# Second attention of a four-layer kernel: another order of its score maxima, with three PSUM banks for them

## The reference

```python
c_kv = hidden_states @ w_dkv.T
q = (hidden_states @ w_q.T).reshape(B, S, HEADS, HEAD_DIM)
k = (c_kv @ w_uk.T).reshape(B, S, HEADS, HEAD_DIM)
v = (c_kv @ w_uv.T).reshape(B, S, HEADS, HEAD_DIM)
scores = jnp.einsum('bqhd,bkhd->bhqk', q, k) * scale
scores = scores + alibi_bias(S)[None, None]
attn = jax.nn.softmax(scores, axis=-1)
out = jnp.einsum('bhqk,bkhd->bqhd', attn, v).reshape(B, S, HIDDEN)
return out @ w_o.T
```

## Time and profile before

| | us |
|---|---|
| median of 3 runs | 3481.03 (3480.75 to 3494.99) |
| profiled execution, its own time | 3483.64 |
| its span | 3482.0 |
| plain scores alone, 19 quads | 2607 to 2662 |
| plain and transposed together | 2662 to 3118 |
| transposed and products alone | 3118 to 3161 |
| PE, DVE, ACT busy, share of the span | 75%, 60%, 46% |
| mean granted clock of PE | 0.819 |

### The profile page before, as it was taken

How to read it: one execution, slowest core, us unless ns; L and a number is a source line. 1 busy time by engine, 2 the same in 40 slices (tenths; PEclk the granted TensorE clock), 3 DMA queues, 4 the chain that set the end, 5 groups by cost and what they waited for, 6 DMA issues and landing times. The chain is left out here.

```text
span 3482.0 us, 45060 instructions
## 1 busy us (share of the span) xinstructions
PE 2622.4 (75%) x12496; PEld 1651.7 (47%) x12497; DVE 2087.5 (60%) x4677; ACT 1584.9 (46%) x2875; POOL 465.3 (13%) x758
## 2 busy tenths in 40 slices
PE   5991069601689989998999999588249999997693
PEld 2330023201467767775777677455124444444452
DVE  3338953598267767775777777532317776763422
ACT  2446324660256555664655566223112666664231
POOL 0220012100011111101111110031300000000314
PEclk8555555555699999999999999789675999998797
DMA  3000000001300000000000000222270022000123
GB/s 98 0 0 0 0 0 0 0 0 39 110 10 7 7 9 9 7 6 11 7 7 7 10 7 1 73 80 78 67 172 8 2 37 37 1 1 2 61 82 100
DMA packets 82226, 100.62 MB, mean 29 GB/s; under 512 B 24931, under 2 KB 71619, under 8 KB 79043
## 3 DMA queue, kind: packets, MB, share of 16 engines
q1 hardware_dynamic: 69476, 70.45, 7.8%
q0 software_dynamic: 12544, 27.68, 2.5%
HBM read 60.99 MB, written 36.70 MB: 28 GB/s over the span
## 5 line engine op out<-in xcount | busy, mean ns | idle before, releaser
L1122 ACT ACTIVATE aa_pt_hi<-psum 128x512 fp32r<-128x512 f32 x544 | 322.3, 595 | 343.5 <-PE psum L1028 342.8
L1662 DVE TENSOR_REDUCE ab_part_max<-psum 128x1 f32<-128x512 f32 (+3 forms) x640 | 364.2, 607 | 177.4 <-PE psum L1500 172.7
L1184 DVE TENSOR_TENSOR aa_pt_lo<-psum,aa_pt_hi 128x512 fp32r<-128x512 f32 x544 | 368.1, 687 | 39.6 <-ACT aa_pt_hi L1122 38.8
L1604 ACT ACTIVATE ab_prob<-psum 128x512 f32<-128x512 f32 (+3 forms) x640 | 303.5, 537 | 165.3 <-PE psum L1529 161.9
L1171 DVE CUSTOM_DVE_ANT_0 aa_prob<-psum,bias 128x512 f32<-128x512 f32 (+2 forms) x480 | 284.1, 597 | 108.1 <-PE psum L1018 102.4
L1500 PE MATMUL psum<-ab_k_stack,ab_q_stack 49*128 49x512 f32 (+3 forms) x640 | 285.4, 489 | 26.4 <-DVE ab_part_max L1662 25.8
L973 POOL TENSOR_TENSOR aa_tmp<-aa_q_nat,rope 128x128 f32<-128x128 f32 x256 | 109.1, 458 | 1294.7 <-ACT aa_q_nat L1099 1294.7
L1016 PE MATMUL psum<-ka_hi,aa_q_hi 128*128 128x512 f32 (+3 forms) x640 | 272.9, 426 | 9.2 <-DVE aa_chunk_max L1171 8.0
L1039 PE MATMUL psum<-aa_pt_hi,c_stack 128*128 128x512 f32 x544 | 271.5, 499 | 2.6 <-DVE aa_pt_lo L1184 2.6
L1028 PE MATMUL psum<-ident,aa_prob 128*128 128x128 f32 x1600 | 264.7, 273 | 10.2 <-ACT aa_prob L1114 5.6
L504 PE MATMUL psum<-ix_bad_row,mean 128*128 128x1 f32 x4 | 1.2, 363 | 340.9 <-DVE ix_bad_row L631 340.9
(11 more groups left out here) (343 smaller groups left out, 4980.7 us busy)
## 6 DMA issues: line engine op xcount, KB each, us to landing
f_rows_in<-sent SPq DMA_DIRECT2D x80, 128.0 KB, 2.0
done<-f_rows_out POOLq DMA_DIRECT2D x80, 128.0 KB, 2.0
aa_xt<-xT_rows SPq DMA_DIRECT2D x64, 128.0 KB, 2.4
w<-in_w SPq DMA_DIRECT2D x6, 896.0 KB, 7.2
sent<-ixp_zeros SPq DMA_DIRECT2D x4, 1280.0 KB, 10.4
x<-in_hidden SPq DMA_DIRECT2D x2, 2048.0 KB, 9.1
ab_q_stack<-stash_q_hi SPq DMA_DIRECT2D x32, 128.0 KB, 9.9
ab_k_stack<-stash_k_hi SPq DMA_DIRECT2D x32, 128.0 KB, 11.2
```

The costliest lines, as they stand in the source:

```text
L1122: nc.scalar.activation(pt_hi[(TB[t] + j) % RING][:], turn_bank[(TB[t] + j) % RING], ACT.Copy).then_inc(pt_hi_done, 1)
L1184: nc.vector.tensor_tensor(pt_lo[ring][:], turn_bank[(TB[t] + j) % RING], pt_hi[ring][:].bitcast(F32), ALU.subtract).then_inc(pt_lo_done, 1)
L1604: nc.scalar.activation(prob[i % 2][h][:, 0:w], t_bank[slot % RING][:, 0:w], ACT.Exp).then_inc(t_taken, 1)
L1662: nc.vector.tensor_reduce(part_max[e % 2][:, 4 * h + t % 4, part:part + 1], s_bank[piece % 2][:, 0:w], AX.X, ALU.max).then_inc(s_used, 1)
```

## The change

The order is written anew. Plain scores no longer run a fixed 19 quads ahead but one event ahead: while the transposed quads of event e are worked on, the plain quads of event e + 1 are issued. `wanted(i)` spreads them evenly over the first quads of the event, and leaves the last three (AHEAD = 3; two in an event of four quads) for the way of the maxima; in those it lets at most two quads of event e + 2 begin. The turn of an event's maxima comes at the end of the step after the one in which its last plain score was issued. Where a step has more than four fresh pieces, the surplus is issued after its four transposed scores, ahead of the products of the quad before.

Even groups take their chunks upward (4, 8, 12, 16 quads), odd ones downward (16, 12, 8, 4), so that neighbouring events are of like size. Ahead of the first transposed score stand the plain scores of event 0 and of half of event 1, then the turn of event 0.

The plain scores have three banks and the results one. The first `weigh` of an event now waits for `keep` of the event just before.

```diff
-    RING = 4
-    LEAD = 19
+    RING, S_RING = 4, 3
+    AHEAD = 3
+    EVENT = [(g, c) for g in range(NG) for c in (range(NCH) if g % 2 == 0 else reversed(range(NCH)))]
...
-        for m in range(LEAD):
-            steps += scores(m) + turns(m - 1)
+        def wanted(i):
+            e = T_QUADS[i][0]
+            if e + 1 == EVENTS:
+                return ALL
+            room = SIZE[e] - min(AHEAD, SIZE[e] // 2)
+            more = -(-(i - FIRST[e] + 1) * SIZE[e + 1] // room)
+            return FIRST[e + 1] + min(more, SIZE[e + 1] + AHEAD - 1)
+        turned = 0
+        steps += scores(SIZE[0])
         for i in range(ALL + 3):
-            fresh = scores(i + LEAD)
+            ready = issued
+            fresh = scores(wanted(i)) if i < ALL else []
+            if i == 0:
+                steps += fresh + [("turn", 0)]
+                turned, ready, fresh = 1, 0, []
             for h in range(GB):
                 if i < ALL:
                     steps.append(("t", i, h))
                 steps += fresh[h:h + 1]
+            steps += fresh[GB:]
             if 1 <= i <= ALL:
                 steps += [("weigh", i - 1, h) for h in range(GB)]
...
-            steps += turns(i + LEAD - 1)
+            if turned < EVENTS and FIRST[turned + 1] <= ready:
+                steps.append(("turn", turned))
+                turned += 1
...
-        s_bank, t_bank, o_bank = bank[0:2], bank[2:2 + RING], bank[6:8]
+        s_bank, t_bank, o_bank = bank[0:S_RING], bank[S_RING:S_RING + RING], bank[7]
...
-                    if piece >= 2:
-                        pe.wait_ge(s_used, piece - 1)
+                    if piece >= S_RING:
+                        pe.wait_ge(s_used, piece - S_RING + 1)
...
-                    if kb == 0 and h == 0 and e >= 2:
-                        pe.wait_ge(kept, e - 1)
+                    if kb == 0 and h == 0 and e:
+                        pe.wait_ge(kept, e)
```

More of the change, by code:

```diff
@@ L1348, in attention_b, with scores @@
     DEEP, LATE = 4, 5
-    RING = 4
-    LEAD = 19
[L1352 to L1357, removed]
-    def order():
[L1363 to L1369, removed]
-        for m in range(LEAD):
-            steps += scores(m) + turns(m - 1)
-        for i in range(ALL + 3):
-            fresh = scores(i + LEAD)
+    RING, S_RING = 4, 3
+    AHEAD = 3
+    EVENT = [(g, c) for g in range(NG) for c in (range(NCH) if g % 2 == 0 else reversed(range(NCH)))]
+    EVENTS = len(EVENT)
+    SIZE = [4 * (c + 1) for _, c in EVENT]
+    FIRST = [sum(SIZE[:e]) for e in range(EVENTS + 1)]
+    T_QUADS = [(e, g, c, kb) for e, (g, c) in enumerate(EVENT) for kb in range(4 * (c + 1))]
+    S_QUADS = [(e, g, t, part) for e, (g, c) in enumerate(EVENT) for t in range(4 * c, 4 * c + 4) for part in range(c + 1)]
+    ALL = len(T_QUADS)
+    NQ = ALL // NG
+    EVENT_ENDING = {FIRST[e + 1] - 1: e for e in range(EVENTS)}
+    def order():
+        steps, issued = [], 0
+        def scores(upto):
+            nonlocal issued
+            fresh = []
+            while issued < min(upto, ALL):
+                fresh += [("s", issued, h) for h in (1, 0, 3, 2)]
+                issued += 1
+            return fresh
+        def wanted(i):
[7 more added lines that the diff above has]
+        steps += scores(SIZE[0])
+        for i in range(ALL + 3):
+            ready = issued
[3 more added lines that the diff above has]
+                turned, ready, fresh = 1, 0, []
             for h in range(GB):
@@ L1378, in order @@
                 steps += fresh[h:h + 1]
+            steps += fresh[GB:]
             if 1 <= i <= ALL:
                 steps += [("weigh", i - 1, h) for h in range(GB)]
-                if (i - 1) % NQ in ENDS:
-                    steps.append(("keep", (i - 1) // NQ * NCH + ENDS.index((i - 1) % NQ)))
-            steps += turns(i + LEAD - 1)
-            if i >= 2 and (i - 2) % NQ in ENDS and (i - 2) // NQ < NG:
-                steps.append(("flip", (i - 2) // NQ * NCH + ENDS.index((i - 2) % NQ)))
+                if i - 1 in EVENT_ENDING:
+                    steps.append(("keep", EVENT_ENDING[i - 1]))
+            if turned < EVENTS and FIRST[turned + 1] <= ready:
+                steps.append(("turn", turned))
+                turned += 1
+            if i >= 2 and i - 2 in EVENT_ENDING:
+                steps.append(("flip", EVENT_ENDING[i - 2]))
         return steps
@@ L1474, in _ @@
                 for e in range(EVENTS):
-                    g, c = divmod(e, NCH)
+                    g, c = EVENT[e]
                     pool.wait_ge(t_taken, SLOT[("turn", e)] + 1)
@@ L1484, in score @@
                 def score(m, h):
-                    g, (t, part) = m // NQ, S_QUADS[m % NQ]
+                    e, g, t, part = S_QUADS[m]
                     w, piece = min(CH, (t + 1) * P - part * CH), PIECE[("s", m, h)]
-                    out, at = s_bank[piece % 2], slice(base(h), base(h) + R_MAX)
+                    out, at = s_bank[piece % S_RING], slice(base(h), base(h) + R_MAX)
                     q, k = q_stack[g % 2][h // 2], k_stack[g % 2][h // 2]
@@ L1511, in transposed_score @@
                 def transposed_score(i, h):
-                    g, (c, kb) = i // NQ, T_QUADS[i % NQ]
+                    e, g, c, kb = T_QUADS[i]
                     q0 = max(c * CH, kb * P)
@@ L1518, in transposed_score @@
                     if kb == 0 and h == 0:
-                        e = g * NCH + c
                         pe.wait_ge(max_in[e % 2], (e // 2 + 1) * GB * 16)
@@ L1532, in weigh @@
                 def weigh(i, h):
-                    g, (c, kb) = i // NQ, T_QUADS[i % NQ]
-                    e, q0 = g * NCH + c, max(c * CH, kb * P)
+                    e, g, c, kb = T_QUADS[i]
+                    q0 = max(c * CH, kb * P)
                     w = (c + 1) * CH - q0
                     pe.wait_ge(t_taken, SLOT[("t", i, h)] + 1)
-                    if kb == 0 and h == 0 and e >= 2:
-                        pe.wait_ge(kept, e - 1)
+                    if kb == 0 and h == 0 and e:
+                        pe.wait_ge(kept, e)
                     at = q0 - c * CH
-                    last = nc.tensor.matmul(o_bank[e % 2][32 * h:32 * h + DHB + 1, at:at + w], values[:, g * GB + h, kb, :],
+                    last = nc.tensor.matmul(o_bank[32 * h:32 * h + DHB + 1, at:at + w], values[:, g * GB + h, kb, :],
                                             prob[i % 2][h][:, 0:w], start=kb == 0, stop=kb == 4 * c + 3,
@@ L1564, in out_tile @@
                     last.then_inc(out_done, 1)
-                pe.wait_ge(after_set, 4)
+                pe.wait_ge(after_set, 3)
                 pe.wait_ge(same_in, 2 * SAME_ROWS * 16)
@@ L1597, in exponential @@
                 def exponential(i, h):
-                    c, kb = T_QUADS[i % NQ]
+                    e, g, c, kb = T_QUADS[i]
                     w, slot = (c + 1) * CH - max(c * CH, kb * P), SLOT[("t", i, h)]
@@ L1615, in keep @@
                 def keep(e):
-                    g, c = divmod(e, NCH)
-                    act.wait_ge(pv_done, g * NQ + ENDS[c] + 1)
+                    act.wait_ge(pv_done, FIRST[e + 1])
                     if e >= 2:
                         act.wait_ge(t_ready, SLOT[("flip", e - 2)] + 1)
-                    nc.scalar.activation(o_rows[e % 2][:], o_bank[e % 2], ACT.Copy).then_inc(kept, 1)
+                    nc.scalar.activation(o_rows[e % 2][:], o_bank, ACT.Copy).then_inc(kept, 1)
                 def store_sums(e):
-                    (g, c), slot = divmod(e, NCH), SLOT[("flip", e)]
+                    (g, c), slot = EVENT[e], SLOT[("flip", e)]
                     act.wait_ge(t_ready, slot + 1)
@@ L1629, in store_sums @@
                                          ACT.Copy).then_inc(t_taken, 1)
-                act.wait_ge(after_set, 4)
+                act.wait_ge(after_set, 3)
                 for what in STEPS:
@@ L1652, in _ @@
                 nc.vector.tensor_copy(halves[:], prob[0][1][:, 0:2 * P].rearrange("p (a n) -> p a n", a=2)).then_inc(after_set, 1)
-                for p in range(2):
-                    nc.vector.memset(o_bank[p], 0.0).then_inc(after_set, 1)
+                nc.vector.memset(o_bank, 0.0).then_inc(after_set, 1)
                 def maxima(m, h):
-                    (t, part), piece = S_QUADS[m % NQ], PIECE[("s", m, h)]
-                    e = m // NQ * NCH + t // 4
+                    (e, g, t, part), piece = S_QUADS[m], PIECE[("s", m, h)]
                     w = min(CH, (t + 1) * P - part * CH)
                     dve.wait_ge(s_ready, piece + 1)
-                    nc.vector.tensor_reduce(part_max[e % 2][:, 4 * h + t % 4, part:part + 1], s_bank[piece % 2][:, 0:w],
+                    nc.vector.tensor_reduce(part_max[e % 2][:, 4 * h + t % 4, part:part + 1], s_bank[piece % S_RING][:, 0:w],
                                             AX.X, ALU.max).then_inc(s_used, 1)
-                    if m % NQ in ENDS and h == 2:
+                    if m in EVENT_ENDING and h == 2:
```

## The result

The changed kernel takes 3502.54 us (median of 11 runs, 3494.26 to 3515.38), the kernel before 3483.57 in its 11. The ratio is 1.006, 95% interval 1.0043 to 1.0077: slower by 0.6%, 15 to 27 us. The profiled execution took 3507.04 us with a span of 3505.4.

The account below looks back on a forecast made before the run. PE and DVE hand two banks to and fro, neither full. After the start, 469.8 + 18 + 2.5 + 9 + 35 = 534 us against 499, begun 35 us earlier: change 0, 3480 us, range 3447 to 3512.

Parts of the forecast that it names:

- the clock: PE's clock in the phase: 111 us at half, costing 35 us, against 57 us costing 18 before.
- My prices of the steps: Steps after the start, priced by plain pieces and transposed width at full clock: 469.8 us in sum.
- 9 us of boundaries: Fifteen flips and turns between events cost PE 0.6 us each: 9 us, between 0 and 19.
- the nine waits for maxima: PE waits bare before events, 1.5 us six times and 3.0 three times; 8 us at half clock for each.
- The second rival: The clock stays down in the up-going runs of events: 3505 us, chance 0.15.
- The start: Plain scores ahead of the first transposed score: it comes at about 2626.5, 35.1 us earlier.
- A quad with three banks: Full step with one plain quad: 2.68 us in place of 3.33, as the third piece no longer waits.
- DVE-bound steps: Steps with two or more plain quads: DVE sets the pace, 2.58 us each plus 0.1.
- The rival that the bank does not help: The 44 one-quad steps stay at 3.33 us, costing 29 us more: 3509 us, chance 0.09.
- The count of the order: Steps priced by event: upward 18.4, 32.5, 43.8, 46.5 us, then downward 38.7, 28.0, 17.4, 11.7 in the first two groups.
- The way of the maxima: The 4.25 us from turn to transposed score, partly bare before nine events: 18 us together, plus 2.5 for a stage's DMAs.
- One result bank: Costs nothing, since products of the next event come late enough; without that cover 0.6 us x 15.

Follow-up runs that it names:

- the run with a lead of 17: Kernel before with three banks for plain scores and one for results, plain scores 17 quads ahead in place of 19: 3394.10 us, ratio 0.9769.
- Bursts: Old order, three banks for plain scores, 19 quads ahead, but two plain quads in every other step and none between: 3507.97 us in one run, against 3473.84 before.
- the two kernels with one plain quad a step: Three banks for plain scores, fixed 19 quads ahead: in the old order 3389.21 us, with the changed kernel's turned chunk order 3370.52 us.
- the experiment with the bank alone: Kernel before with three banks for plain scores and one for results, order untouched: 3389.21 us, ratio 0.9711.
- four banks: Four banks for plain scores, three for transposed ones, 19 quads ahead: old order 3386.67 us, even groups upward and odd ones downward 3381.02 us.
- three ways to put more work into PE: Changed kernel with off-diagonal plain scores' matmuls doubled: 3530.68 us; only 112 surplus ones: 3495.64 us; those 112 with an added 128-row matmul instead: 3520.99 us.
- all plain scores twice: Changed kernel with the matmul of each plain score off the diagonal issued twice into the same bank: 3530.68 us, ratio 1.0111.
- even groups, four banks: Even groups upward, odd ones downward, 19 quads ahead, four banks for plain scores and three for transposed ones: 3381.02 us, ratio 0.9735.
- these stacks were held back: Changed kernel, but DMAs bringing group 3's stacks wait until the maxima of event 9 have landed: 3504.61 us, ratio 1.0034.

## Why the prediction was wrong

I forecast no change, 3480 us, and it is 19 us slower. The step that failed is **the clock**: the prediction took 111 us at half, costing 35. There were 230. The price of 0.32 for a microsecond at half was near enough. My prices of the steps, 9 us of boundaries and 17 of waits leave 61 us of the 557 for the clock, 0.27 each. Steps of one kind, sorted by their plain pieces and the width of their transposed scores and set side by side at the two clocks, give 0.31 (55 us for 178 at half). So the 230 us cost some 60 to 70, an estimate. The term is 25 to 35 us short, and that is the miss.

I had tied the falls to the nine waits for maxima, because the fall that I looked at, at 3126, stood behind one. It was not the only one in the profile before. The earlier trace rows themselves lie in another, and in the 12 us ahead of that one PE never waited longer than 0.4 us:

```profile
2930.00:2935.00 5.00, 4.41 (x44) 2.54 (x37) 4.11 (x7) 2.13 (x7) 0.00 (x0) 1.00 1.03 129
2935.00:2949.00 14.00, 13.93 (x55) 5.99 (x54) 7.71 (x14) 7.40 (x15) 2.05 (x4) 0.51 0.97 124
```

The tie itself is real, and the run with a lead of 17 shows it. It is not the main one. In the changed kernel six of the nine waits came about; behind two of them (ends at 2743.8 and 2798.5) the clock stayed at 1.00, and at 2922 it had fallen before the wait of 9 us began. Bursts with hardly a wait lose the clock just the same, and the two kernels with one plain quad a step and hardly a wait keep it at 0.99. The second rival, the clock staying down in upward runs, named the place and came within 3 us (3505 against 3502.5); I gave it 0.15. It took 35 steps with plain scores at half there, and the trace has 31 that spent most of their time so. Its argument, a stage of plain scores alone that never left 0.50, was in the first group of rows, and I did not let it into my own sum.

The other terms, one by one:

- **The start**: 2626.5 forecast, 2626.2 measured. The gain of 35 us is right.
- **A quad with three banks**: 2.68 forecast, 2.73 measured. DVE-bound steps 5.26 forecast, 5.10 measured. (The counts in the prediction add up to 158 steps; two or more plain quads stand in 37, not 35.) The rival that the bank does not help fell, and the experiment with the bank alone puts it at 100 us.
- **The count of the order**: downward events at full clock took 28.6 and 18.2 us where I had 28.0 and 17.4 (from `keep` to `keep`, with a flip and a turn in each); the upward ones 52.8 and 54.7 for 43.8 and 46.5, which is the clock, and 1.0 and 1.2 of wait.
- **The way of the maxima**: 18 us and 2.5 for the stage. PE stood 21.1 us for these DMAs in all (15.1 and 6.0 in the two groups of the waits); without the first turn's 4.0 that is 17. But 9.0 of them are one wait, beside group 3's stacks, for which I had 3.0 and 2.5. Of the other eight only five came about, and together cost 8 us, not 15: what lies between them hides more than I allowed.
- **One result bank**: free, as forecast.

What I did not do is the greater lesson. The same prices, put on the old order with three banks, sum to 402 us of steps and 40 of start, where the new order has 468 and 15 (measured 40 and 20, since the first maxima now come bare). Written side by side, these two sums say that the order loses 41 us before any clock is counted, and that the gain is all in the bank. I set the change only against the old kernel, whose two banks hid what its order was worth.

**What stays open** is what in an uneven step lets the clock fall. Shown: bursts alone take it from 0.99 to 0.82 (one run), in the old chunk order, and the change has 0.79. An even spread is not enough to keep it: with a lead of 17 and its four waits it is 0.94, and with four banks it fell in the stretch without plain scores. Of three ways to put more work into PE two raised it, to 0.83, and none paid. Whether it is the thin stretch behind the transposed scores, the step without plain scores that follows, or their alternation was not told apart. All clock figures are from one profiled execution of each kernel. Nor was it tried to fill the steps without plain scores.

## What to carry to other kernels

Where two engines hand buffers to and fro, with a wait in every step and neither engine full, try one more buffer, and try that part alone first: here it was worth 100 us. Where a fast and a slow kind of work are paired, keep their ratio the same in every step: here uneven steps lost the pairing twice, once in the time and once in PE's clock. A lead that looks like waste at both ends (40 and 39 us here) can be what keeps the middle even, and what covers the longest wait: two quads less of it laid 15 us of waits bare, with a fall of the clock behind each.

## What the runs showed of the hardware

The granted clock reacts to how evenly PE's work comes, and not only to how much of it there is. PE's busy share after the start, as the profile models it, says little: the two kernels with the clock at 0.99 have 98%, but below that 97% goes with 0.83 (all plain scores twice) and 95% with 0.94 (even groups, four banks). A wait of 3.7 us was followed by a fall all four times with a lead of 17. Without any such wait the clock fell when the plain scores had ended in the kernels with four banks for them, for 60 and 34 us.

What half clock costs differs by step. A full step without plain scores took 2.07 us at full clock (three banks for plain scores, ACT busy 35 of 39 us in that stretch) and 4.04 at half (four banks, PE busy 57 of 60 us); a step with two plain quads, which DVE's 4.87 us of pieces bound, took 5.10 and 6.56.

Small DMAs on one queue land later beside large ones on another: 8.9 us to landing for 2 KB beside group stacks, 1.5 us without. Once these stacks were held back, none took over 2.8 us.
